# Exponentials by a polynomial in five stages, and GpSimd's indirect DMAs tied to the scan's states

## What is computed

```python
A_bar = expm(dt_A * A)                      # 64 x 64
def step(state, bc):
    b_t, c_t = bc
    s = state @ A_bar + b_t
    s = _layernorm(s, ln_st_g, ln_st_b)
    return (s, c_t * s)
_, ys = jax.lax.scan(step, state0, ...)      # 512 steps
ssm = transpose(ys) @ D_w.T + D_b
s = ssm * gate

topw, topi = jax.lax.top_k(logits, 2)        # of 8 experts
h = gelu(einsum('bsd,edh->ebsh', xn, ew1) + eb1)
eo = einsum('ebsh,ehd->ebsd', h, ew2) + eb2
moe_out = einsum('ebsd,bse->bsd', eo, w_dense)
for i in range(3):
    moe_out = moe_out @ expm(gens[i])        # 128 x 128 each
mixed = abel_out * (1.0 - g) + moe_out * g
x = x + s * silu(xn + mixed)
```

## Time and profile before

| | us |
|---|---|
| median of 3 runs | 578.85 |
| lowest, highest | 575.68, 583.21 |
| the profiled execution, measured | 579.03 |
| its traced span | 577.1 |
| PE busy | 363.4 (63%) |
| VectorE busy | 296.5 (51%) |
| ScalarE busy | 203.8 (35%) |
| GpSimd busy | 149.3 (26%) |
| granted TensorE clock, mean | 0.784 of full speed |

### The profile page before, as it was taken

The page is one execution under the profiler, slowest core; times in us unless marked ns, Lnnn a source line. Parts: engine busy times, 40 slices in busy tenths (PEclk is TensorE's granted clock), DMA queues, the critical chain, the costliest instruction groups (busy, mean ns, idle before and its releaser), DMA issues.

```text
span 577.1 us, 11969 instructions
## 1 busy us (share of the span) xinstructions
PE 363.4 (63%) x4243; PEld 258.7 (45%) x4243; DVE 296.5 (51%) x1378; ACT 203.8 (35%) x577; POOL 149.3 (26%) x187
## 2 busy tenths in 40 slices
PE   2879886200105999989999423884778720976870
PEld 1769563100003666677767213753557400333550
DVE  4883794000003477778866202563788500663794
ACT  0348330000001243465655202762776400543500
POOL 4310016777750000000000671005000374022133
PEclk9989588555555599999999855898899955895865
DMA  7291003113110000074748422715434221001022
GB/s 251 73 334 30 0 3 124 50 55 109 52 43 1 0 1 0 23 264 171 264 149 268 127 55 62 262 65 180 134 106 168 56 56 37 2 15 25 2 76 74
DMA packets 52680, 54.34 MB, mean 94 GB/s; under 512 B 6649, under 2 KB 38560, under 8 KB 52640
## 3 DMA queue, kind: packets, MB, share of 16 engines
q1 hardware_dynamic: 37695, 38.21, 19.6%
q0 software_dynamic: 4096, 8.43, 5.1%
q10 hardware_dynamic: 10848, 7.25, 4.1%
HBM read 14.11 MB, written 16.56 MB: 53 GB/s over the span
## 4 chain that ended last, share of the span: by engine, by line
PE 37%; another core or an unknown queue 27%; DVE 24%; ACT 4%; issue 3%; DMA 3%; SPq 1%; DVEq 0%; ACTq 0%
PE bank L1049 9%; PE bank L365 5%; PE bank L1395 4%; DVE xpad L1186 3%; PE bank L1404 3%; DVE ring L953 2%; DVE wT L941 2%; PE bank L1377 2%; PE bank L1368 2%; PE bank L1361 2%; DMA record<-experts 2%; PE bank L398 1%; PE bank L438 1%; DVE gi L1195 1%
## 5 line engine op out<-in xcount | busy, mean ns | idle before, releaser
L1049 PE MATMUL bank<-Mrep,wT 32*32 32x64 f32 x2560 | 74.4, 234 | 162.4 <-DVE wT L941 93.7
L1049 PEld LDWEIGHTS bank<-Mrep,wT 32*32 32x32 f32 x2560 | 47.8, 112 | 217.3 <-issue 216.3
L1629 POOL DMA_INDIRECT pulls<-expert_rows,slots x64 | 60.7, 948 | 293.6 <-DMA expert_rows<-rows_out 203.0
L953 DVE SCALAR_TENSOR_TENSOR ring<-bank,Rho,Dv 128x64 f32<-128x64 f32 x124 | 35.2, 284 | 153.0 <-remote 107.9
L1498 ACT ACTIVATE desk<-bank,record 128x128 f32<-128x128 f32 x156 | 48.8, 364 | 67.9 <-PE bank L1395 41.4
L1616 POOL DMA_INDIRECT sorted_rows<-late,slots x64 | 61.9, 968 | 27.3 <-issue 19.2
L1395 PE MATMUL bank<-desk,record 128*128 128x128 f32 x312 | 57.7, 309 | 2.0 <-DMA record<-experts 2.0
L1404 PE MATMUL bank<-record,desk 128*128 128x129 f32 x312 | 51.2, 288 | 6.3 <-ACT desk L1498 4.1
L365 PE MATMUL bank<-bias,ones 128*128 128x512 bf16 x165 | 52.9, 426 | 0.0
L1404 PEld LDWEIGHTS bank<-record,desk 128*128 128x128 f32 x312 | 43.1, 200 | 8.5 <-issue 7.9
L1395 PEld LDWEIGHTS bank<-desk,record 128*128 128x128 f32 x312 | 42.4, 197 | 9.6 <-issue 2.4
(11 more groups left out here) (308 smaller groups left out, 655.3 us busy)
## 6 DMA issues: line engine op xcount, KB each, us to landing
record<-experts SPq DMA_DIRECT2D x78, 290.5 KB
sorted_rows<-zero_rows SPq DMA_DIRECT2D x2, 2496.0 KB, 17.5
expert_rows<-rows_out ACTq DMA_DIRECT2D x12, 322.5 KB, 4.6
desk<-sorted_rows SPq DMA_DIRECT2D x12, 320.0 KB
X<-in_L_attn_x ACTq DMA_DIRECT2D x4, 512.0 KB, 6.7
out<-experts SPq DMA_DIRECT2D x8, 256.0 KB, 2.1
expert_rows<-rows_out ACTq DMA_DIRECT2D x6, 193.5 KB, 3.2
desk<-sorted_rows SPq DMA_DIRECT2D x6, 192.0 KB
```

The costliest lines, as they stand in the source:

```text
L953: dve.scalar_tensor_tensor(out=state(r, k), in0=psY, scalar=Rho[:, k:k + 1], in1=Dv[:, k, :], op0=ALU.mult, op1=ALU.add).then_inc(sem("sta ...
L1049: t = pe.matmul(psY[q], wT[q, 32 * c:32 * c + 32], Mrep[q, c, :], start=(c == 0), stop=(c == 1))
L1629: pool.indirect_dma_start(pulls[:, n % 3, j, s, :], None, expert_rows[n // (NB // HALVES)], bass.IndirectOffsetOnAxis(ap=slots[:, j, q:q + ...
```

## The change

Two parts.

**The polynomial.** The Taylor polynomial up to the tenth power is split by powers of three. X squared and the square's transpose are made first, then X cubed, then three products by X cubed: six four-products in place of nine, each but the first two behind one pass of VectorE. It is built for the transposed matrices (`ET`); the transposes of line 458 and ScalarE's first copy now make `EX` from it. VectorE's list between the stages is dealt out anew: `norm_statistics(1)`, `(2)` and `z_tile(0)` come behind the last stage, `z_tile(1)` into the first squaring; PE's `z_transposes(0)` comes behind the first squares.

**The pacing.** A scatter past the tenth waits for one state each: the one with number i of the 64 waits for step i - 10 of the sweeps (`scan_turn` turns a count of steps into a value of `state`). The gathers of tiles 0 to 3 wait for steps 80 to 111, those of tiles 4 to 7 for steps 124 to 155. The mixes of tiles 0 to 3 move to other steps, and the third part of each on ScalarE comes 9 steps behind the first in place of 13.

```diff
-            for k in range(TAYLOR - 1, 0, -1):
-                pe.wait_ge(sem("taylor"), TAYLOR - k)
+            def four_products(bank, left, right):
                 for m in range(4):
-                    t = pe.matmul(banks[1][:, m * P:(m + 1) * P], XT[:, m, :], EX[:, m, :], start=True, stop=True)
+                    t = pe.matmul(banks[bank][:, m * P:(m + 1) * P], left[:, m, :], right[:, m, :], start=True, stop=True)
                 t.then_inc(sem("taylor_product"), 1)
...
+            pe.wait_ge(sem("expm_arg"), 1)
+            four_products(1, XT, XE)
+            four_products(2, XE, XT)
...
+            pe.wait_ge(sem("taylor"), 2)
+            four_products(1, XT, EX)
+            ew2_transposes(0)
+            ew2_transposes(1)
+            pe.wait_ge(sem("taylor"), 3)
+            four_products(1, EX, ET)
+            ew2_transposes(2)
+            pe.wait_ge(sem("taylor"), 4)
+            four_products(1, EX, ET)
+            ew2_transposes(3)
+            pe.wait_ge(sem("taylor"), 5)
+            four_products(1, EX, ET)
...
+            pe.wait_ge(sem("taylor"), 6)
             for m in range(4):
-                t = pe.transpose(banks[2][:, m * P:(m + 1) * P], EX[:, m, :], ident[:, :])
+                t = pe.transpose(banks[2][:, m * P:(m + 1) * P], ET[:, m, :], ident[:, :])
...
-            z_transposes(0)
...
+                if k == 0:
+                    z_transposes(0)
...
-                act.copy(ET[:, :, :], banks[2][:, :].rearrange("p (m n) -> p m n", m=4)).then_inc(sem("squared_T"), 1)
+                act.copy((ET if k else EX)[:, :, :], banks[2][:, :].rearrange("p (m n) -> p m n", m=4)).then_inc(sem("squared_T"), 1)
...
+            dve.scalar_tensor_tensor(out=ET, in0=XT, scalar=1.0 / 10, in1=ident4, op0=ALU.mult, op1=ALU.add).then_inc(sem("taylor"), 1)
+            dve.scalar_tensor_tensor(out=high, in0=XT, scalar=1.0 / 7, in1=ident4, op0=ALU.mult, op1=ALU.add)
+            dve.scalar_tensor_tensor(out=mid, in0=XT, scalar=1.0 / 4, in1=ident4, op0=ALU.mult, op1=ALU.add)
+            dve.tensor_tensor(low, XT, ident4, ALU.add)
+            dve.wait_ge(sem("taylor_product"), 1)
+            dve.tensor_copy(EX, product).then_inc(sem("taylor"), 1)
+            stats(0)
...
+            dve.scalar_tensor_tensor(out=high, in0=squares, scalar=1.0 / 56, in1=high, op0=ALU.mult, op1=ALU.add)
+            dve.wait_ge(sem("taylor_product"), 3)
+            dve.tensor_copy(EX, product).then_inc(sem("taylor"), 1)
+            dve.scalar_tensor_tensor(out=mid, in0=squares, scalar=1.0 / 20, in1=mid, op0=ALU.mult, op1=ALU.add)
+            dve.scalar_tensor_tensor(out=low, in0=squares, scalar=1.0 / 2, in1=low, op0=ALU.mult, op1=ALU.add)
+            stats(1)
+            stats(2)
...
+            dve.scalar_tensor_tensor(out=ET, in0=product, scalar=1.0 / 504, in1=high, op0=ALU.mult, op1=ALU.add).then_inc(sem("taylor"), 1)
+            for n in range(3, 6):
+                stats(n)
...
+            dve.scalar_tensor_tensor(out=ET, in0=product, scalar=1.0 / 120, in1=mid, op0=ALU.mult, op1=ALU.add).then_inc(sem("taylor"), 1)
+            stats(6)
+            stats(7)
+            norm_statistics(0)
...
+            dve.scalar_tensor_tensor(out=ET, in0=product, scalar=1.0 / 6, in1=low, op0=ALU.mult, op1=ALU.add).then_inc(sem("taylor"), 1)
+            norm_statistics(1)
+            norm_statistics(2)
+            z_tile(0)
...
-        ACT_MIX = {91: 0, 98: 1, 105: 2, 113: 3}
-        DVE_MIX = {100: 0, 107: 1, 114: 2, 122: 3}
+        ACT_MIX = {93: 0, 101: 1, 109: 2, 117: 3}
+        DVE_MIX = {97: 0, 105: 1, 113: 2, 121: 3}
         FIRST_LATE = 8
+        UNPACED = 10
+        GATHERS = 80
+        LATE_GATHERS = 4 * L - 4
...
-                        for part, late_by in enumerate((0, 1, 13)):
+                        for part, late_by in enumerate((0, 1, 9)):
...
+                def scan_turn(step):
+                    return step + 1 + step // L
+
                 def scatter(h):
                     for q in range(h * Q, (h + 1) * Q):
                         for j in range(2):
+                            at = (q * 2 + j) - UNPACED
+                            if at >= 0:
+                                pool.wait_ge(sem("state"), scan_turn(at))
...
                             q = n * SUB + s
+                            pool.wait_ge(sem("state"), scan_turn((LATE_GATHERS if n >= NB // HALVES else GATHERS) + (q % Q) * 2 + j))
```

More of the change, by code:

```diff
@@ L15 @@
 SCALE_STEPS = 5
-TAYLOR = 10
 UNROLL = 8
@@ L447, in front_tensor @@
-                if 4 <= k <= 7:
-                    ew2_transposes(7 - k)
-                if k == 3:
-                    pe.wait_ge(sem("weights_loaded"), 16 * N_W)
-                    pe.transpose(banks[7][:, 464:464 + E], eb2[:, :], ident[0:E, 0:E])
-                    pe.transpose(banks[7][:, 480:480 + E * K], eb1_rows[:, :], ident[0:E * K, 0:E * K])
-                    pe.matmul(banks[7][:, 0:2 * P], ones[0:1, :], gc_w_row, start=True, stop=True)
-                    pe.matmul(banks[7][:, 2 * P:2 * P + E], ones[0:1, :], mgb_row, start=True, stop=True)
-                    pe.matmul(banks[7][:, 2 * P + E:2 * P + E + 1], ones[0:1, :], gc_b_row, start=True, stop=True).then_inc(sem("rows_all"), 1)
@@ L456, in front_tensor @@
-            pe.wait_ge(sem("taylor"), TAYLOR)
+            pe.wait_ge(sem("expm_arg"), 1)
+            four_products(1, XT, XE)
+            four_products(2, XE, XT)
+            pe.wait_ge(sem("matrices_loaded"), 80)
+            for j in range(2):
+                pe.transpose(banks[0][:, j * P:(j + 1) * P], gate_w[:, j, :], ident[:, :])
+            for j in range(2):
+                pe.transpose(banks[0][:, 2 * P + j * S:2 * P + (j + 1) * S], BC_w[:, j, :], ident[0:S, 0:S])
+            pe.transpose(banks[0][:, 384:512], D_w[:, :, :].rearrange("p j n -> p (j n)"), ident[:, :]).then_inc(sem("small_T"), 1)
@@ new lines, in front_tensor @@
+            pe.transpose(banks[7][:, 464:464 + E], eb2[:, :], ident[0:E, 0:E])
+            pe.transpose(banks[7][:, 480:480 + E * K], eb1_rows[:, :], ident[0:E * K, 0:E * K])
+            pe.matmul(banks[7][:, 0:2 * P], ones[0:1, :], gc_w_row, start=True, stop=True)
+            pe.matmul(banks[7][:, 2 * P:2 * P + E], ones[0:1, :], mgb_row, start=True, stop=True)
+            pe.matmul(banks[7][:, 2 * P + E:2 * P + E + 1], ones[0:1, :], gc_b_row, start=True, stop=True).then_inc(sem("rows_all"), 1)
@@ L735, in front_vector @@
             dve.wait_ge(sem("expm_arg"), 1)
-            dve.scalar_tensor_tensor(out=EX, in0=XE, scalar=1.0 / TAYLOR, in1=ident4, op0=ALU.mult, op1=ALU.add).then_inc(sem("taylor"), 1)
-            for k in range(TAYLOR - 1, 0, -1):
-                if k >= 6:
-                    stats(2 * (9 - k))
-                    stats(2 * (9 - k) + 1)
-                elif k >= 3:
-                    norm_statistics(5 - k)
-                elif k == 2:
-                    z_tile(0)
-                else:
-                    z_tile(1)
-                dve.wait_ge(sem("taylor_product"), TAYLOR - k)
-                dve.scalar_tensor_tensor(out=EX, in0=banks[1][:, :].rearrange("p (m n) -> p m n", m=4), scalar=1.0 / k, in1=ident4,
-                                         op0=ALU.mult, op1=ALU.add).then_inc(sem("taylor"), 1)
+            low, mid, high = (records[:, i * 512:(i + 1) * 512].rearrange("p (m n) -> p m n", m=4) for i in range(3))
@@ new lines, in front_vector @@
+            product, squares = (banks[i][:, :].rearrange("p (m n) -> p m n", m=4) for i in (1, 2))
+            dve.scalar_tensor_tensor(out=ET, in0=XT, scalar=1.0 / 10, in1=ident4, op0=ALU.mult, op1=ALU.add).then_inc(sem("taylor"), 1)
+            dve.scalar_tensor_tensor(out=high, in0=XT, scalar=1.0 / 7, in1=ident4, op0=ALU.mult, op1=ALU.add)
+            dve.scalar_tensor_tensor(out=mid, in0=XT, scalar=1.0 / 4, in1=ident4, op0=ALU.mult, op1=ALU.add)
+            dve.tensor_tensor(low, XT, ident4, ALU.add)
@@ L754, in front_vector @@
             for k in range(SCALE_STEPS):
+                if k == 0:
+                    z_tile(1)
                 if k < 3:
```

15 lines of the change are left out of this document (8 added, 7 removed).

## The result

Four runs of the kernel after took 481.0 to 484.85 us, median 483.11; four of the kernel before, run beside them, 575.68 to 585.23, median 581.03. The ratio is 0.834, with a 95% interval of 0.826 to 0.842. The forecast was 480 us. A second job (a set of runs made together, the kernel before among them) with the same kernel gave 481.48 us against 576.54 (0.835, 0.833 to 0.838).

A forecast was written before the change was run, and what follows sets the result against it. The bound was taken as the scan's serial chain of state, transpose, product and next state, stopped by bursts of indirect DMAs. 577.1 - 91.3 (stalls) - 8 (clock) - 0 (polynomial) = 477.8, with 1.9 around it 480 us; range 420 to 560.

The forecast's parts named there:

- The cause: In the scan, bursts of GpSimd's indirect DMAs delay the news of PE's finished product: 128 DMAs go with 154.1 us of stall.
- The unpaced ten: First scatters of the scan, free of a wait: first product seen at about 104.0 in place of 95.6, 8.4 us lost.
- The short burst: Four or five gathers already due when the second half's rows land go out together: 5 x 1.20 = 6 us.
- The paced ones in round 4: Last round of the scan: product seen no earlier than 1.67 us after its state; 27 x 0.69 = 18.6 us.
- The paced ones in rounds 0 to 3: Early rounds of the scan: each paced DMA costs 0.35 us, 85 x 0.35 = 29.8 us, none hidden by mixing steps.
- The clock: With PE fed, the scan's groups of steps at 1.2 GHz go: 8 us gained, bounds 0 and 17; PEclk 9 through round 0.
- The end of round 0: The scan's first round should end near 165 us in place of 236.
- The share of no engine: Part of the chain put down to no engine: from 27% to some 13%, no piece over 15 us after the first product.
- The polynomial: Ahead of the scan: transposed result 4.9 us earlier, little of it arriving; taken as 0, bounds -1.5 (slower) and 2.4 us.
- Absorbed: Rival: a lone indirect DMA in the scan costs nothing, only bursts choke; gain 139.7 us, time 430 us; chance 0.23.
- Nothing gained: Rival: each indirect DMA costs its 1.20 us wherever it stands in the scan; gain 5.3 us, time 574; chance 0.09.
- slower: Rival: the 1.94 us tail after a burst belongs to each lone DMA too; time 655 us; chance 0.08.

The follow-up runs named there:

- e1_no_pacing: The kernel after without the waits of GpSimd's scatters and gathers on the scan's states; polynomial and moved mixes kept: 581.27 us, ratio 1.005 to before.
- e2_no_poly: The kernel before with only the pacing waits and the moved mixing steps, the old polynomial kept: 483.55 us, ratio 0.836.
- e11_mixed: The kernel after with scatters in three forms: plain DMAs from SyncE, plain from GpSimd, indirect ones of 16 bytes per row: 452.24 us, ratio 0.785.
- e4_narrow: The kernel after with each of its 64 scatters writing 16 bytes per row instead of 512: 423.04 us, where before took 414.85 us.
- e8_none: The kernel after without its 128 scatters and gathers, semaphores raised: 413.99 us, 0.998 of before, which took 414.85 us in that job.

## Why the prediction was right

The mechanism was right, and the sum came out at 480 against 483 because most of its terms did.

- *The cause.* The bursts of indirect DMAs hold the news of PE's product. e1_no_pacing and e2_no_poly show that it is the pacing that counts, e11_mixed that it is GpSimd's indirect DMAs and no others. Why they do it, and why not in every job, is not shown. By the Trainium skill's page "SBUF — State Buffer", section "Who interferes with whom", DMA never contends with a compute engine. In the jobs with the hold the traces disagree: the compute engines' chain stops beside GpSimd's issues, until 1.40 us after each lone one. In the job without it the times agree: e4_narrow, paced, took 1.024 of before and gained nothing.
- *The unpaced ten.* Forecast: first product at about 104.0; seen at 104.20 here, at 103.53 to 106.50 in the other traces with ten unpaced, the pacing and the hold, so that the hit to 0.2 us is luck. The loss of 8.4 us was real: with five it shrank by 5.9. The tail behind the last unpaced scatter was 2.1 us (102.08 to 104.20), forecast 1.94.
- *The short burst.* Forecast: five gathers once, 6 us. There were two: five back to back at 267.24 to 272.27, and seven at 379.71 to 387.20, with gaps of no engine of 4.74 and 3.05 + 3.45 us. 11.2 us in place of 6. The step that failed is the one that took the rows' landing to be late once; after pacing it is late in both halves.
- *The paced ones in round 4.* Forecast: 1.67 us after the state's end, so a step of 0.28 + 1.67 = 1.95. Measured 1.93 to 2.00 in 16 of the 31 steps, some 0.69 over the 1.26 without one.
- *The paced ones in rounds 0 to 3.* Forecast: 1.60 becomes 1.95. Measured 1.96 to 2.00 in most steps of round 0, 1.97 to 2.34 in those of round 1. But an undisturbed step of round 0 is 1.57 (e11_mixed, with 1.35 and 1.76 in turn), so the term there is 0.4 and not 0.35. Round 1 lost 31 x (1.91 - 1.62) = 9.0 us to 22 scatters, 0.41 each, where 7.7 was forecast. In round 3 the cover that was counted at nothing exists: 2.35 against 2.27 a step with no DMAs, 2.5 us for 16 gathers against the 5.6 forecast, since its mixing steps are long anyway. Over all rounds the kernel after stands 31 x (0.54 + 0.29 + 0.33 + 0.08 + 0.65) = 58.6 us over the means of e8_none, bursts behind the first product included (e8_none is of the job without the hold); the forecast for the same was 48.4 + 6 = 54.4.
- *The clock.* Forecast: 8 us, PEclk at 9 through round 0. Wrong in its reason. The granted clock of round 0 rose from 0.64 to 0.79 only:

```profile
104.00:120.00 16.00, 13.37 (x177) 8.96 (x177) 9.37 (x56) 5.04 (x10) 7.51 (x8) 0.82 0.08 30
120.00:125.00 5.00, 5.00 (x31) 2.67 (x32) 2.36 (x14) 0.70 (x2) 2.02 (x3) 0.50 0.10 39
125.00:136.50 11.50, 9.71 (x147) 6.25 (x150) 6.72 (x40) 3.81 (x9) 5.08 (x6) 0.95 0.07 29
```

  Stretches at half clock (1.2 of 2.4 GHz) still come. In windows of half a microsecond the lower level stands from 119.5 to 126, from 136.5 to 143 and from 153.5 to 160, and PE had been busy 84% of the time from 104 to 120 (13.37 of 16.00). Each of the three holds one step of 3.06 to 3.12 us in place of 1.97. At about 1.1 us each the three of round 0 take back 3.4. Since the stalls of before had cost more than their ten pieces (all steps of before stand 31 x (2.47 + 0 + 1.10 + 0.04 + 1.33) = 153.1 us over e8_none, and its first product 13.1 later, 166 in all, against the 154.1 of the pieces), the gain of 8 was nearly there all the same.
- *The end of round 0* came at 169.5 (its last update), forecast 165; the 4 us are the 0.4 for 0.35 and the three slow steps.
- *The share of no engine* was forecast at 13% and is 4%. The paced holds, forecast at 48.4 us, are not shown as pieces of no engine but as part of PE's line (PE bank L1082 makes 21% of the chain), because each ends at a product. The largest piece is 9.57 us, under the 15 forecast.
- *The closeness of the sum.* 480 against 483 is in part luck. The bursts came out 5.2 us dearer than forecast and round 0's slow steps took 3.4 us, while round 3 came out 3.1 cheaper, and the clock's 8 us came from stalls that cost more than their pieces.
- *The polynomial.* Forecast at nothing, and 0.3 us ahead of the scan is what came. Its inner order was as told, its durations not all:

```profile
27.03 0.94 PE L468 MATMUL bank<-ident,desk 128*128 128x128 f32 x4 [2.18 <-DVE desk L777]
...
37.51 0.78 ACT L558 ACTIVATE xpad<-bank,cols 128x512 f32<-128x512 f32 x1 [4.79 <-PE bank L373]
38.85 0.58 ACT L607 COPY desk<-bank 128x512 f32<-128x512 f32 x1
```

  The transposes of the exponential start at 27.03, forecast 29.6: later four-products take 1.06 to 1.16 us, not the 2.07 of the early ones on which the step was costed. It changes nothing: affine(0) stands at 37.51 (forecast 37.8) and ScalarE's second copy at 38.85 (forecast 39.2; before 39.14).
- *The rivals.* "Absorbed" (430) was wrong for pacing by the state (483); pacing by the product (447 with five unpaced) comes nearer to it. "Nothing gained" and "slower" fall with 0.4 us a paced DMA, far from the 1.25 at which the second decides. A rival that was not on the list is the job without the hold, where before takes 415 us and the nearest kernel measured was 2.4% slower.

## What to carry to other kernels

When a chain between PE and VectorE stops with both idle and nothing to wait for, look at what GpSimd issues at that moment, and look at one isolated issue: its hold ended at a fixed time after it, so the place in the step to which it is paced decides what it costs. Here waiting for the product (0.17 us into the step) instead of the state (0.56) was worth 31 us, as much as a third of the pacing itself. And run the kernel before beside each candidate, in the same job: a cause that makes 166 us in one can be missing in the next.

## What the runs showed of the hardware that was not expected

- When GpSimd issues a lone indirect DMA of 128 rows (0.94 to 0.96 us), a product of PE that ends meanwhile reaches VectorE about 1.40 us after the issue began (1.42, 1.40, 1.46 above; under 1.35 at only 1 of 98 issues), whether a row is 512 or 16 bytes. ScalarE is held as well (104.24 above). Plain DMAs of GpSimd (0.54 us) and of SyncE delay nothing here. The first scatters can let a product through earlier: in the kernel before one was taken at 93.51, 0.92 us after the issue at 92.59, and nothing here says why. Behind eleven back to back the next product is seen 2.12 us after the last issue's end, behind eight 1.94.
- This is so in some jobs only. Five had it (before at 581.0, 576.2, 576.5, 576.5 and 574.8 us); one had not (414.85 us), with the same duration of issue. What differs stays open: nothing in the traces names it, and the chip number on record is the same, 0, for the job without it and for one of the five.
- The clock falls to its lower level in three stretches of some 6.5 us in round 0, with PE busy 84% ahead of the first, and not only behind stalls.
